# Order of the search units, a first turn of maxima inside the Q, K, V stage, and three norm orders of a two-layer kernel

## What is computed

```python
x = L0_attn_x                                              # 1 x 1024 x 512
x = _layernorm(x + _L0_attn_ref(x, ...))                   # selective state-space scan
x = _layernorm(x + _L0_ffn_ref(x, W_gate, W_up, W_down))   # silu(x Wg) * (x Wu), then Wd; 1792 wide
x = _layernorm(x + _L1_attn_ref(x, wq, wk, wv, wo))        # 32 heads of 16, rotary, causal softmax
x = _layernorm(x + _L1_ffn_ref(x, gate_*, up_*, down_*))   # the same with 4-bit weights; 1376 wide
# the attention:
scores = jnp.einsum('bnth,bnsh->bnts', q, k) * (1.0 / math.sqrt(h))
scores = jnp.where(causal, scores, -jnp.inf)
attn = jax.nn.softmax(scores, axis=-1)
out = jnp.einsum('bnts,bnsh->bnth', attn, v)
```

## Time and profile before

| | us |
|---|---|
| median of 3 runs | 879.1 |
| lowest, highest | 876.25, 879.51 |
| the profiled execution | 876.1 |
| its span, first to last instruction | 874.4 |

### The profile page before, as it was taken

The page is one execution under the profiler, slowest core; times in us unless marked ns, Lnnn a source line. Parts: engine busy times, 40 slices in busy tenths (PEclk is TensorE's granted clock), DMA queues, the critical chain, the costliest instruction groups (busy, mean ns, idle before and its releaser), DMA issues.

```text
span 874.4 us, 19489 instructions
## 1 busy us (share of the span) xinstructions
PE 804.1 (92%) x8137; PEld 383.5 (44%) x8137; DVE 642.1 (73%) x900; ACT 443.5 (51%) x584; POOL 301.8 (35%) x217
## 2 busy tenths in 40 slices
PE   7669787787999999999989999999989999999997
PEld 2434344444444444455544444444424444444443
DVE  4999999997565333444669999999976677775344
ACT  4976666546654321254427777777786433332100
POOL 0699899991001000155421222121143222221000
PEclk9589999999999999999988999999999999999999
DMA  6900000005230000000000000000132013330001
GB/s 215 365 3 3 3 3 2 3 4 168 97 115 1 1 0 1 1 1 1 1 1 2 2 2 2 2 2 3 37 115 86 1 59 118 123 110 0 13 36 48
DMA packets 20017, 38.25 MB, mean 44 GB/s; under 512 B 5009, under 2 KB 10961, under 8 KB 19938
## 3 DMA queue, kind: packets, MB, share of 16 engines
q1 hardware_dynamic: 19938, 37.10, 12.4%
HBM read 34.87 MB, written 2.16 MB: 42 GB/s over the span
## 4 chain that ended last, share of the span: by engine, by line
PE 76%; DVE 13%; issue 4%; POOL 3%; ACT 2%; DMA 1%; SPq 1%; DVEq 0%; ACTq 0%; POOLq 0%
PE ps L832 13%; PE ps L613 11%; PE ps L590 10%; PE ps L769 8%; DVE arena L1354 7%; PE ps L702 7%; PE ps L867 7%; PE ps L666 6%; PE ps L753 3%; PE ps L706 3%; POOL arena L1205 2%; PE ps L679 2%; PE ps L509 2%; PE ps L465 1%; PE ps L778 1%
## 5 line engine op out<-in xcount | busy, mean ns | idle before, releaser
L1563 DVE TENSOR_REDUCE arena<-ps 128x1 f16<-128x512 f32 (+3 forms) x320 | 181.4, 630 | 6.4 <-PE ps L706 4.1
L1114 ACT ACTIVATE arena<-ps 128x1024 f32<-128x1024 f32 (+2 forms) x160 | 143.4, 940 | 60.6 <-PE ps L753 58.8
L1205 POOL TENSOR_TENSOR arena<-arena 128x1024 f32<-128x1024 f32 x62 | 152.0, 2485 | 9.3 <-DVE arena L1354 8.9
L1354 DVE TENSOR_TENSOR_SCAN arena<-arena,ps 128x1024 f32<-128x1024 f32 x64 | 142.1, 2269 | 2.0 <-PE ps L509 1.7
L832 PE MATMUL ps<-arena 128*128 128x512 f16 x528 | 114.5, 379 | 1.4 <-DVE arena L1671 1.4
L702 PE MATMUL ps<-arena 64*128 64x512 f16 (+3 forms) x384 | 99.6, 339 | 0.7
L1254 POOL TENSOR_SCALAR_AFFINE_SELECT arena<-arena 128x512 f32<-128x512 f32 x64 | 43.4, 685 | 162.4 <-ACT arena L1114 162.3
L613 PE MATMUL ps<-arena 128*128 128x512 f16 x448 | 97.5, 379 | 1.5 <-DVE arena L1494 1.5
L957 ACT ACTIVATE arena<-arena,negA 128x1024 f32<-128x1024 f32 x64 | 72.8, 1146 | 45.4 <-DVE arena L1354 43.2
L509 PE MATMUL ps<-arena 64*128 64x64 f16 x3072 | 60.0, 196 | 35.1 <-DVE arena L1354 31.8
L509 PEld LDWEIGHTS ps<-arena 64*128 64x128 f16 x3072 | 52.2, 98 | 86.3 <-DVE arena L1354 75.0
(11 more groups left out here) (173 smaller groups left out, 973.1 us busy)
## 6 DMA issues: line engine op xcount, KB each, us to landing
arena<-in_w_q_dram SPq DMA_DIRECT2D x11, 768.0 KB, 4.2
arena<-c_rows SPq DMA_DIRECT2D x16, 512.0 KB, 10.7
arena<-in_w_s_dram SPq DMA_DIRECT2D x11, 384.0 KB, 4.9
arena<-in_x_fm_dram SPq DMA_DIRECT2D x8, 256.0 KB, 4.3
out_dram<-arena SPq DMA_DIRECT2D x8, 256.0 KB, 2.0
arena<-in_wg_dram SPq DMA_DIRECT2D x1, 1792.0 KB, 10.2
arena<-in_wu_dram SPq DMA_DIRECT2D x1, 1792.0 KB, 7.3
arena<-in_wd_dram SPq DMA_DIRECT2D x1, 1792.0 KB, 11.3
```

The lines of the kernel that those rows point to most:

```text
L1114: nc.scalar.activation(dst, src, ACT.Exp, scale=float(HD) ** -0.5).then_inc(exp_done, 1)
L1205: nc.gpsimd.tensor_tensor(hC[i % 4][:], hst[i % 3][:], c_all[:, n, :], ALU.mult).then_inc(hc_done, 1)
L1354: nc.vector.tensor_tensor_scan(hst[i % 3][:], dA[i % 3][:], banks(2 * (i % 2), 2), 0.0, ALU.mult, ALU.add).then_inc(scan_done, 1)
L1563: nc.vector.reduce_max(maxima_slot(half, k), ps[:, ring_bank(n), 0:len(heads) * w].rearrange("p (a w) -> p a w", a=len(heads)), AX, negate ...
```

## The change

- The turn of the maxima of group 0, first half, moves from the head of the attention into the Q, K, V stage: tile step t = 6, place 1, ahead of two search units (`EARLY_TURN` = 14). Its copy goes to `keep_rows` in the same place on VectorE. `m_row` and `z_nib` swap their addresses.
- The search units of both halves are taken in a fixed new order (`UNIT_ORDER`), and the early ones are sorted by tile.
- `PATTERN` and `START` are other ones, with the same counts of letters. Searches lead by 41 instead of 36 units, keys by 3 steps.
- `searched` names the count after which a half is searched, wherever its last unit now stands.
- The first `nibbles` and `unscaled` stand behind the last turn step instead of the out step.
- `gate_up0(0)` is cut in two halves of 256 tokens; the first waits for two tiles instead of four.
- In the third norm TensorE, ScalarE and VectorE walk another order, and the first up product is cut by chunks around `second_turn(7)`.
- In the last norm tile 6 is finished before tile 7, and tile 7 is made in two halves of 256 columns in two banks.

```diff
-        m_row = view(192, T, f16)
+        m_row = view(196, T, f16)
+        UNIT_ORDER = ((0, 1, 6, 8, 7, 3, 2, 9, 4, 11, 10, 5),
+                      (15, 4, 17, 13, 24, 5, 19, 26, 27, 12, 7, 10, 3, 8, 25, 20, 6, 9, 14, 0, 2, 21, 22, 11, 16, 1, 23, 18))
+        SEARCH = [[max_units(half)[k] for k in UNIT_ORDER[half]] for half in range(2)]
+        EARLY_UNITS = [(half, k) for i in range(EARLY_TILES) for half in range(2) for k, unit in enumerate(SEARCH[half]) if unit[0] == i]
+        EARLY_TURN = len(max_units(0)) + 2
+        EARLY_UNITS.insert(EARLY_TURN, None)
...
+            return ([EARLY_TURN] if (t, place) == (6, 1) else []) + units[2 * place:2 * place + 2]
...
-        PATTERN = ("sskkssvvnssskktossvsksksssksksnvsskvsks"
-                   "vssksktosksvskssksvskkssvssksvssskvsskv")
-        START = {'s': 36, 'k': 0, 't': 1, 'o': -1, 'v': -2, 'n': 1}
+        PATTERN = ("sksktsvssksosvsskkssnvskssvsksktvsskssk"
+                   "svskssvsskoksvsksksvskkssvsskkssvssknvs")
+        START = {'k': 3, 'v': -1, 's': 41, 'n': 2, 't': 1, 'o': -1}
...
+                    if not turn:
+                        produce(TT - 2, 0, False)
+                        pe.wait_ge(ln_taken, TT * (ln - 1) + TT - 2)
+                        make(TT - 1, 1, 0, D // 2).then_inc(last_half, 1)
+                        make(TT - 1, 2, D // 2, D).then_inc(ln_in, 1)
...
+            pe.wait_ge(xl_done, TT // 4)
+            gate_up0(0, 0, HALF // 2)
             pe.wait_ge(xl_done, TT // 2)
-            gate_up0(0)
+            gate_up0(0, HALF // 2, HALF)
...
             second_turn(4)
-            second_turn(5)
             pe.wait_ge(w1_low, 1)
             pe.wait_ge(xl_done, 2 * TT + TT // 2)
             gate_up1(0, 0, (0,), first=True, only=(0,))
+            second_turn(5)
             second_turn(6)
             pe.wait_ge(ln_taken, TT + 7)
-            gate_up1(0, 0, (0,), first=True, only=(1,))
+            gate_up1(0, 0, (0,), first=True, only=(1,), chunks=(0, 1))
             second_turn(7)
+            gate_up1(0, 0, (0,), first=True, only=(1,), chunks=(2, 3))
...
             for t in range(TT - 2):
+                second_high(t)
                 if t + 3 < TT:
                     second_root(t + 3)
                 second_normalise(t + 2)
-                second_high(t)
...
+                if not turn:
+                    dve.wait_ge(x_normed, TT * ln + TT - 2)
+                    root_taken(TT - 2, 0)
+                    normalise(TT - 2, 0)
+                    dve.wait_ge(last_half, 1)
+                    take_last(1, 0, D // 2)
+                    dve.wait_ge(ln_in, TT * ln + TT)
+                    take_last(2, D // 2, D)
...
-            for t in range(TT):
+            second_shift(0)
+            second_stats(2)
+            second_shift(1)
+            for t in range(2, TT - 1):
+                second_stats(t + 1)
+                second_low(t - 2)
                 second_shift(t)
-                if t + 2 < TT:
-                    second_stats(t + 2)
-                if t >= 2:
-                    second_low(t - 2)
+            second_shift(TT - 1)
+            second_low(TT - 3)
             second_low(TT - 2)
             second_low(TT - 1)
```

111 lines of the change are left out of this document (69 added, 42 removed).

## The result

| | before | changed kernel |
|---|---|---|
| median | 876.18 (17 runs) | 873.12 (17 runs) |
| lowest, highest | 873.99, 879.51 | 871.88, 877.25 |
| profiled execution, span | 876.1, 874.4 | 875.27, 873.5 |

The ratio is 0.9958, with a 95% interval of 0.9945 to 0.9970: 3.7 us (2.6 to 4.8) faster, and by the bound of 0.5% just "within". The change is real and small. Of its 17 executions thirteen took 871.88 to 873.5 us at a mean granted clock of 0.967 to 0.971 and four took 875.15 to 877.25 us at 0.963 to 0.966, and the profiled one (0.965) is of the four. It differs from the profiled execution of before by only 0.9 us, so each stretch is read by itself.

What follows compares the result with a forecast made beforehand. TensorE was taken to bound the second feed-forward part, VectorE's maxima the attention groups and ScalarE's exponentials its end. Terms 0 + 2.0 - 0.5 - 2.4 - 0.5 - 3.4 - 1.3 = -6.1 us gave 873.0 from 879.1, range 868.5 to 879.0.

Steps and rivals of the forecast that it cites:

- What bounds the attention: Attention groups: VectorE's maxima bound them, 24.87 us in a group of 25.62, with TensorE close behind at 23.7.
- First product: First gate product in two halves: TensorE gets ahead by about 1.4 us, yet gains 0; bounds 0 and -1.4.
- the Silu named: Third Silu on ScalarE, 229.08 to 229.68, for which the fifth gate unit already waits 0.22 us; expected no earlier.
- Early turn: Tile step 6: a search unit waits for the copy behind keep_keys, +2.0 us; attention's head saves 0.5.
- Pattern: Attention groups under the new step pattern: VectorE's marked wait goes, 7.35 x 0.33, -2.4 us; bounds -5.6 and +3.7.
- the marked wait: In each attention group, one VectorE wait of 0.34 us marked as TensorE's, taken as gone in the new pattern.
- VectorE's 24.87 us a group stay: Attention groups: the work is the same, so VectorE's busy time was to stay and only idle time could go.
- The dry ring: Rival, chance 0.07: TensorE late at values steps, 1.8 us more per group, total +9.5 us, 888.6.
- End of attention: After the last maxima: ScalarE's chain starts a little earlier and isn't held by values, -0.5 us.
- a divide that nobody waits for: End of attention: moved nibbles delay only a divide not needed until the last output, hidden by exponentials, 0.
- Third norm: From last output projection to full TensorE: new order removes waits of 2.11 and 1.40 us, -3.4; worse bound -1.4.
- Last norm: Chain behind the last matmul, 3.93 us: half steps shorten it to 2.68, taken as -1.3; bounds -0.8 and -1.5.

Runs made afterwards that it cites:

- unit order and pattern alone: Two kernels: the kernel before with only the new search unit order (ratio 1.0098), and with only the new pattern and its starts (ratio 1.0091).
- order and pattern only: Kernel before with the search units' new order and the new pattern with its starts, nothing else; ratio 0.9989, median 875.82 us.
- the pattern only: Kernel before with the new pattern and its starts, search units in their old order; ratio 1.0091, median 882.46 us.
- weights first: Changed kernel with VectorE's weight preparation ahead of the divide of the seventh group's half 0, instead of behind it; ratio 0.9932, median 870.36 us.
- copy ahead: Changed kernel with the early turn's copy ahead of keep_keys(5) on VectorE instead of behind it; ratio 0.9932, median 870.32 us.

## Why the prediction was right or wrong

The predicted time was 873.0, the median is 873.12, but that they agree is luck, since two errors cancel. The sum was made against a median of before of 879.1 from three runs; seventeen runs give 876.18. And the change was forecast at -6.1 us and measured at -3.7 (the two medians differ by 3.06). The chance for faster by over 0.5% was the largest, and the 0.42% lies within. Point by point:

- *What bounds the attention*: right. VectorE's maxima with TensorE close behind; how close, unit order and pattern alone show, since small reorderings make TensorE late.
- *First product, 0*: right, by the Silu named.
- *Early turn, +2.0, head -0.5*: the mechanism was right, and nearly the size: 2.15 us for the turn where 1.9 was forecast, and 0.23 ahead of it where the new unit order got 0.1. The equal 435.17 is partly luck, by the mark's 0.42. Up to the first maxima the turn costs the same 2.14, if the clock is alike; the profile's +3.01 holds 0.62 of half clock besides, and 0.25 are there without the early turn too. The head gave the 0.5.
- *Pattern, -2.4*: the value was close (-2.73 with order and pattern only, -1.86 in the changed kernel's profile), and the term was right in its mechanism: the marked wait is gone, 0.34 us a group, -2.1 in six groups. But I spread it over 7.35 groups, while it exists in six; opening and end lose 0.9. What makes up for this was not in the sum: "VectorE's 24.87 us a group stay" failed, since the join no longer stands beside a mask, -1.5 in six groups. So groups came out at 25.02, not at 25.3, just above the 25.0 below which I had called the prediction wrong. The Trainium skill (TensorEngine Tiling (Array Packing), Key Properties) has a change of tiling mode drain TensorE, by which the new group, with 31 changes, would have been 25.7 us at most. It is 25.02, so no drain of a size that matters here is seen, and the 26.48 of the pattern only, with the same 31 changes, is not made of them.
- *The dry ring*, my slower rival at 0.07, names a mechanism that is there: it cost 0.85 us a group with the pattern alone. The new unit order removes it, and I had not looked at that order for anything but partitions.
- *End of attention, -0.5 with bounds of 0 and -1.2*: this step failed, by 3.2 us. I followed the second half's keys and the moved `nibbles`, and not the work behind out 7.0, which moved 4 us towards the end with the pattern; "a divide that nobody waits for" was said of the step in front, and the next divide was the one that stood in the way. What it cost is 1.14 us of wait and, in the changed kernel's profile, 1.98 of half clock beside the transposes. With that work moved the tail is 25.70, 0.65 less than before, near what the term said.
- *Third norm, -3.4*: -3.28, and kept to the end in every kernel.
- *Last norm, -1.3*: -1.1.

Not settled: how long the half clock of the opening typically is in the changed kernel. Its profile shows 20.4 us; two kernels with the turn in the same place (weights first, copy ahead) show 13.7. Most of the 17 executions have a mean granted clock of 0.967 to 0.971, against 0.965 in the profile, so they had less half clock; where, it doesn't say. With 13.7 us in the opening, and a last `turn_stack` at full clock, the profiled execution would be 1.45 + 0.62 = 2.07 us shorter, about its distance of 2.15 from the median. That is a sum that fits, and not shown; the half clock in the tail can differ too (6.8 us in the changed kernel and three others, 3.4 with copy ahead).

## What to carry to other kernels

When steps of a fixed order move, follow what hangs behind each moved step on the other engines, and not only the step: preparation that once filled a wait can end up in front of the last result. A step put in early costs what the next user of its buffer waits for, so look for a place where the next user is far and both engines wait anyway; here that turned +2.1 us into 0. And an order of units and the pattern that interleaves them are one edit: each alone was 1% slower, together 0.6 us a group faster. Of that 0.25 came from a 128x16 instruction that had stood beside a GpSimd mask: when steps move, look at what lies beside the small ones too.

## What the runs showed of the hardware

- With searches that wait for VectorE (TensorE busy 1.59 of 2 us) the granted clock fell from 1.00 to 0.50 even when TensorE had been kept busy until then, and 14 more matmuls of 512 columns between them kept it at 1.00.
- The same idle time had either effect: behind 1.46 us of idling in tile step 6 the clock stayed at 1.00 in one profile and was 0.50 for 3.4 us in another; before the transposes of `o` 0.88 us of idling was followed by 1.00 in one and by 0.50 in another.
- VectorE's weight preparation was slower in the later place, where GpSimd's masks (L1281, from 657.47 to 661.84) lie beside it: 1.53, 1.11, 0.89 and 0.98 us for steps that took 1.23, 0.69, 0.57 and 0.56 in the earlier one. The join of the maxima took 0.42 us in the 18 groups where a mask (L1254 in before) had started 0.23 us ahead of it, and 0.17 in 24 where none had.
